# Three tiles of 128 rows in place of four in two input projections

## The reference, cut to what matters

```
# layer 0, per pixel                            # layer 1, per image
xn = layer_norm(x, ln1_w, ln1_b)                xn = normalise x in groups of channels over the image
xz = einsum('bld,ed->ble', xn, in_proj_w)       xz = W_in.T @ xn + b_in
xm, z = split(xz, 2)                            xm, z = split(xz, 2)
...  y * silu(z)                                ...  y * silu(z)
```

## Time and profile before

| | us |
|---|---|
| median of three runs | 18655.86 |
| lowest and highest run | 18643.19, 18657.38 |
| the profiled execution, from its first to its last instruction | 18660.7 |

### The profile page before, as it was taken

One profiled execution on the slowest core, in us unless ns is written; L12 is line 12 of the kernel. 1 busy time (PEld: TensorE's weight loads), 2 busy tenths in 40 slices (PEclk: granted clock), 3 DMA queues, 4 the chain that ended last, 5 costly groups with the idle time before them and its releaser, 6 DMA issues. The chain is left out here.

```text
span 18660.7 us, 271066 instructions
## 1 busy us (share of the span) xinstructions
PE 16820.2 (90%) x78344; PEld 10186.0 (55%) x78344; DVE 16050.6 (86%) x12158; ACT 15162.6 (81%) x24326; POOL 12567.1 (67%) x6247
## 2 busy tenths in 40 slices
PE   8799998899996798879899999999999999989798
PEld 3355554455552364455566666666666666547374
DVE  3799998899996486479899999999999999879698
ACT  7699996799992555557899999999999999845556
POOL 0099993599990474135799999999999999700101
PEclk9899998899997899999999999999999999999899
DMA  5788886788879677777433333333333333441313
GB/s 175 230 242 245 236 250 208 233 246 237 247 223 249 217 224 222 253 237 277 166 113 112 113 112 119 113 112 113 112 112 114 122 113 113 125 138 54 104 53 101
DMA packets 898273, 3166.02 MB, mean 170 GB/s; under 512 B 145638, under 2 KB 180170, under 8 KB 872140
## 3 DMA queue, kind: packets, MB, share of 16 engines
q1 hardware_dynamic: 817612, 3011.91, 51.1%
q10 hardware_dynamic: 79104, 136.10, 2.4%
HBM read 2342.21 MB, written 805.32 MB: 169 GB/s over the span
## 5 line engine op out<-in xcount | busy, mean ns | idle before, releaser
L1788 DVE TENSOR_TENSOR_SCAN l1s_h<-l1s_da,l1s_pd 128x1024 f32<-128x1024 f32 x3072 | 6778.1, 2268 | 241.5 <-PE l1s_pd L1720 163.4
L1831 ACT ACTIVATE l1s_dm<-l1s_dut,l1s_bt 128x384 f32<-128x384 f32 x7424 | 4056.8, 604 | 74.0 <-PE l1s_pd L1720 73.8
L1814 ACT ACTIVATE l1s_da<-l1s_dl,l1s_a 128x1024 f32<-128x1024 f32 x3072 | 3496.9, 1138 | 32.0 <-DVE l1s_h L1788 31.0
L1720 PE MATMUL l1s_pd<-l1s_id,l1s_dm 128*128 128x128 f32 x22272 | 2967.8, 274 | 36.4 <-DVE l1s_h L1788 33.9
L1720 PEld LDWEIGHTS l1s_pd<-l1s_id,l1s_dm 128*128 128x128 f32 x22272 | 2561.9, 142 | 487.7 <-issue 287.9
L1694 POOL TENSOR_TENSOR l1s_pb<-l1s_h,l1s_cc 128x1024 f32<-128x1024 f32 x1024 | 2517.8, 2459 | 95.0 <-DVE l1s_h L1788 83.4
L1698 POOL TENSOR_TENSOR l1s_pa<-l1s_sm,l1s_cc 128x1024 f32<-128x1024 f32 x1024 | 2433.1, 2376 | 0.0
L1731 PE MATMUL l1s_py<-l1s_pb,l1s_both 128*128 128x512 f32 x4096 | 2157.4, 609 | 197.1 <-POOL l1s_pb L1694 197.1
L1689 POOL TENSOR_TENSOR l1s_sm<-l1s_h 128x1024 f32<-128x1024 f32 x928 | 2203.5, 2374 | 122.8 <-DVE l1s_h L1788 122.6
L1731 PE MATMUL l1s_py<-l1s_pa,l1s_id 128*128 128x512 f32 x4096 | 2113.4, 598 | 0.3 <-POOL l1s_pa L1698 0.3
L2654 POOL TENSOR_TENSOR l0sf_pr<-l0sf_h,l0sf_cc 128x1024 f32<-128x1024 f32 x768 | 1813.8, 2380 | 71.1 <-DVE l0sf_h L2736 54.8
(11 more groups left out here) (318 smaller groups left out, 30375.1 us busy)
## 6 DMA issues: line engine op xcount, KB each, us to landing
l1s_cc<-crows SPq DMA_DIRECT2D x1024, 512.0 KB, 3.7
l0sf_cc<-l0crowsf SPq DMA_DIRECT2D x512, 512.0 KB, 5.5
l0sb_cc<-l0crowsb SPq DMA_DIRECT2D x512, 512.0 KB, 5.5
l0sf_cc<-l0crowsf SPq DMA_DIRECT2D x512, 256.0 KB, 7.1
l0sb_cc<-l0crowsb SPq DMA_DIRECT2D x512, 256.0 KB, 7.1
dls<-l1p_dl SPq DMA_DIRECT2D x192, 512.0 KB, 7.0
duts<-l1p_dut SPq DMA_DIRECT2D x64, 1536.0 KB, 5.9
l1s_dut<-duts SPq DMA_DIRECT2D x64, 1536.0 KB, 7.2
```

Source lines behind the costliest of these rows:

```text
L1720: mm = pe.transpose(pd[:, s % 2, blk * 128:blk * 128 + 128], dm[:, rnd % 2, blk, j * 128:j * 128 + 128], idt[:, :])
L1788: dve.tensor_tensor_scan(h[:, s % 4, :], da[:, j, :], pd[:, s % 2, :], 0.0, ALU.mult, ALU.add)\
L1814: act.activation(da[:, j, :], dl[:, half, j, :], ACT.Exp, scale=a[:, HT * half + j, n:n + 1])\
L1831: ins = act.activation(dm[:, rnd % 2, blk, :], dut[:, half, blk, :], ACT.Identity, scale=bt[:, half, blk, n:n + 1])
```

## The change

Both stages project their 384 rows as three tiles of 128: the first is xm rows 0 to 127, the last is z rows 64 to 191, and the middle one holds xm rows 128 to 191 in its lower 64 partitions and z rows 0 to 63 in its upper 64. Its two halves are taken out of PSUM by different engines.

In layer 0, ACT copies the first tile and applies Silu to the upper half of the second and to the third; the lower half of the second is a new `tensor_copy` on DVE, placed first in DVE's turn. PE's turn has projections 0 and 1, the average of squares, projection 2, the average of the image. The `pp` buffers are taken by (s + q) % 2, since three tiles a turn shift their parity.

```
@@ l0_in_proj
-        out = r.sb("out", [C, 2, 4, HW])
+        out = r.sb("out", [128, 2, 3, HW])
...
+                        to_x, to_z = xmp[s, :, bass.ds(c * HW + PAD, HW)], one(zs, FRAMES * s + c)
+                        for n, (done, at, dst, rows, q) in enumerate((
+                                (evac, 3 * k, to_x[0:DLOW], slice(0, 128), 0),
+                                (evacd, k, to_x[DLOW:DI], slice(0, DHIGH), 1),
+                                (evac, 3 * k + 1, to_z[0:DHIGH], slice(DHIGH, 128), 1),
+                                (evac, 3 * k + 2, to_z[DHIGH:DI], slice(0, 128), 2))):
+                            sp.wait_ge(done, nth(at))
...
                 def project(k, s, q):
-                    pe.wait_ge(evac, nth(4 * k + q - 2))
+                    pe.wait_ge(evac, nth((3 * k - 2, 3 * k - 1, 3 * k)[q]))
+                    if q == 0:
+                        pe.wait_ge(evacd, nth(k - 1))
...
-                        for q in range(2, 4):
-                            project(k, s, q)
+                        project(k, s, 2)
...
                 def turn(c, s):       # DVE
+                    k = c * SEQS + s
+                    if there(k):
+                        dve.wait_ge(proj, nth(3 * k + 1))
+                        dve.wait_ge(s_out[s % 2][1], (k - s % 2) * 8)
+                        dve.tensor_copy(out[0:DHIGH, s % 2, 1, :], pp[0:DHIGH, (s + 1) % 2, :]).then_inc(evacd, 1)
...
-                        for q in range(2):          # ACT
-                            evacuate(k, s, q)
+                        evacuate(k, s, 0, slice(0, 128), ACT.Copy)
...
-                        for q in range(2, 4):
-                            evacuate(k, s, q)
+                        evacuate(k, s, 1, slice(DHIGH, 128), ACT.Silu)
+                        evacuate(k, s, 2, slice(0, 128), ACT.Silu)
```

```
@@ l1_in_proj
-    OUTS = ((0, 128), (128, 128), (256, 128), (384, 64))
...
-                        for q in (0, 1):
-                            dve.wait_ge(proj, nth(4 * k + q))
+                        for q, rows in ((0, slice(0, 128)), (1, slice(0, DHIGH))):
+                            dve.wait_ge(proj, nth(3 * k + q))
...
                     def project(q):
-                        pe.wait_ge(evac, nth(2 * (k - 1) + q % 2))
-                        if q >= 2:
-                            pe.wait_ge(evacd, nth(2 * k + q % 2))
+                        if q < 2:
+                            pe.wait_ge(evac, nth(2 * (k - 1) + q))
+                        if q == 0:
+                            pe.wait_ge(evacd, nth(2 * (k - 1) + 1))
+                        if q == 2:
+                            pe.wait_ge(evacd, nth(2 * k))
...
                         project(2)
-                        project(3)
...
-                        for q in (2, 3):          # ACT
+                        for q, rows in ((1, slice(DHIGH, 128)), (2, slice(0, 128))):
@@ arranged
-    w["W_in"] = cat([wi[:, :DI], wi[:, DLOW:DI], wi[:, DI:]], 1)
-    w["b_in"] = cat([bi[:DI], bi[DLOW:DI], bi[DI:], np.zeros(64, f)]).reshape(4, 128).T
+    w["W_in"], w["b_in"] = wi, bi.reshape(3, 128).T
```

More of the change, by code:

```diff
@@ L178, in turn @@
                     if there(k):
-                        for q in range(4):
-                            sp.wait_ge(evac, nth(4 * k + q))
+                        to_x, to_z = xmp[s, :, bass.ds(c * HW + PAD, HW)], one(zs, FRAMES * s + c)
[5 more added lines that the diff above has]
+                            sp.wait_ge(done, nth(at))
                             sp.sem_inc(passed, 1)
[L182 to L185, removed]
+                            sp.dma_start(dst, out[rows, s % 2, q, :]).then_inc(s_out[s % 2][n], 16)
                         if there(k + SEQS):
@@ L204, in project @@
                 def project(k, s, q):
-                    pe.wait_ge(evac, nth(4 * k + q - 2))
+                    pe.wait_ge(evac, nth((3 * k - 2, 3 * k - 1, 3 * k)[q]))
+                    if q == 0:
+                        pe.wait_ge(evacd, nth(k - 1))
                     for hs in HALVES:
-                        mm = pe.matmul(pp[:, q % 2, hs], wt[:, q * C:(q + 1) * C], xn[:, s % 2, hs], start=True, stop=True)
+                        mm = pe.matmul(pp[:, (s + q) % 2, hs], wt[:, q * 128:q * 128 + 128], xn[:, s % 2, hs], start=True, stop=True)
                     mm.then_inc(proj, 1)
@@ L259, in _, with evacuate @@
                 act.wait_ge(const, nth(1))
[L261 to L264, removed]
+                def evacuate(k, s, q, rows, func):
+                    act.wait_ge(proj, nth(3 * k + q))
+                    act.wait_ge(s_out[s % 2][q + 1 if q else 0], (k - s % 2) * 8)
+                    act.activation(out[rows, s % 2, q, :], pp[rows, (s + q) % 2, :], func).then_inc(evac, 1)
                 def turn(c, s):
@@ L1237, in turn @@
                     if there(k):
-                        for q, (_, m) in enumerate(OUTS):
-                            sp.wait_ge(evacd if q < 2 else evac, nth(2 * k + q % 2))
+                        for n, (done, dst, rows, q) in enumerate((
+                                (evacd, xx[:, 0], slice(0, 128), 0), (evacd, xx[:, 1, 0:DHIGH], slice(0, DHIGH), 1),
+                                (evac, zs[:, 0:DHIGH, :], slice(DHIGH, 128), 1), (evac, zs[:, DHIGH:DI, :], slice(0, 128), 2))):
+                            sp.wait_ge(done, nth(2 * k + n % 2))
                             sp.sem_inc(passed, 1)
-                            dst = (one(xx[:, q], k) if q < 2 else
-                                   one(zs[:, 0:DLOW, :] if q == 2 else zs[:, DLOW:DI, :], k))
-                            sp.dma_start(dst, out[0:m, q, :]).then_inc(s_out[q], 16)
+                            sp.dma_start(one(dst, k), out[rows, q, :]).then_inc(s_out[n], 16)
                 turns(sp, turn, 3, 0, 2)
@@ L1265, in turn @@
                     if there(k):
-                        for q in (0, 1):
-                            dve.wait_ge(proj, nth(4 * k + q))
+                        for q, rows in ((0, slice(0, 128)), (1, slice(0, DHIGH))):
+                            dve.wait_ge(proj, nth(3 * k + q))
                             dve.wait_ge(s_out[q], k * 16)
-                            dve.tensor_scalar(out[:, q, :], pp[:, q % 2, :], bi[:, q:q + 1], None, ALU.add).then_inc(evacd, 1)
+                            dve.tensor_scalar(out[rows, q, :], pp[rows, (s + q) % 2, :], bi[rows, q:q + 1], None, ALU.add)\
+                               .then_inc(evacd, 1)
                     if there(k + 2):
@@ L1290, in project @@
                     def project(q):
-                        at, m = OUTS[q]
                         pe.wait_ge(xnd, nth(k))
-                        pe.wait_ge(evac, nth(2 * (k - 1) + q % 2))
-                        if q >= 2:
-                            pe.wait_ge(evacd, nth(2 * k + q % 2))
+                        if q < 2:
[4 more added lines that the diff above has]
+                            pe.wait_ge(evacd, nth(2 * k))
                         for hs in HALVES:
-                            mm = pe.matmul(pp[0:m, q % 2, hs], wi[:, at:at + m], xc[:, p, hs], start=True, stop=True)
+                            mm = pe.matmul(pp[:, (s + q) % 2, hs], wi[:, q * 128:q * 128 + 128], xc[:, p, hs], start=True, stop=True)
                         mm.then_inc(proj, 1)
@@ L1347, in turn @@
                     if there(k):
-                        for q in (2, 3):
[L1349 to L1352, removed]
+                        for q, rows in ((1, slice(DHIGH, 128)), (2, slice(0, 128))):
+                            act.wait_ge(proj, nth(3 * k + q))
+                            act.wait_ge(s_out[q + 1], k * 16)
+                            act.activation(out[rows, q, :], pp[rows, (s + q) % 2, :], ACT.Silu, bias=bi[rows, q:q + 1])\
+                               .then_inc(evac, 1)
                 turns(act, turn, 2, 0, 2)
```

14 lines of the change are left out of this document (7 added, 7 removed).

## The result

| | before | after |
|---|---|---|
| median, lowest to highest run (five each), us | 18643.19, 18633.34 to 18657.38 | 18720.1, 18686.12 to 18749.57 |
| ratio, 95% interval | | 1.0037, 1.0025 to 1.005 |
| span of the profiled execution, us | 18660.7 | 18747.8 |
| layer 0's input stage, us | 355.6 | 341.9 |
| layer 1's input stage, us | 495.0 | 563.5 |

The account below looks back on a forecast made before the run. Layer 0 was taken as bound by PE work, barely above its wait loop, layer 1 by its wait loop and clock losses. Layer 1's +64 and layer 0's -10 gave +54 on 18660.7, 18715; 18710 for the median, range 18664 to 18738.

Parts of the forecast that it names:

- Layer 0's turn, 10.0: Layer 0's input stage: a turn falls from 10.41 to 10.0 us, a gain of 12 us over 30 turns.
- the loop of waits: Layer 0: average of squares, Ln, Exp, table load, first Silu, next image's projections; 10.0 us a turn without Ln's delay.
- Ln's lateness: Layer 0: Ln waits for ACT's second Copy, 0.35 us a turn, which one Copy fewer removes.
- Layer 0's clock, +4: Layer 0: 1.4 us of PE idle a turn causes two or three clock losses in the stage, +4 us.
- Rival 4: Layer 0 loses the clock on each turn too, +39 - 2 in place of -10: 18757 us; chance 0.10.
- the 1.7 us forecast there: Layer 0's stage end: the last image's projections have four passes fewer on the path, 1.7 us gained.
- DVE's copy, 1.28, hidden: Layer 0: the new DVE copy takes 1.28 us, hidden because the multiply behind it waits for Exp.
- Layer 1's instructions, no gain of their own: Layer 1: four passes, 1.72 us a turn, go from beside the loop; only 1.7 us gained, in the last turn.
- Layer 1's clock, +2.8 on each of 29 turns: Layer 1: 3.7 us nearly idle on the PE loses the clock every turn; +66 us, +64 after the end gain.
- Rival 1: Layer 1: every turn loses the clock, but for 3.4 us only; +22 in all, 18678 us; chance 0.14.
- rival 2: Layer 1's clock holds as before, nine losses in 29 turns; 18642 us, not slower; chance 0.14.
- Rival 3: Both input stages: PE work is the bound, each removed pass comes off the time, 107 us; 18549 us; chance 0.04.

Follow-up runs that it names:

- The kernel with five products a turn: Changed kernel plus five unneeded 384-column matmuls per layer 1 turn, in the PE's idle time: 18718.36 us, ratio 1.0034 to before; layer 1's stage 479.2 us.
- the kernel with the Silu moved: Changed kernel with layer 1's table load and 64-row Silu ahead of ACT's accumulating sum: 18569.08 us, ratio 0.9964 to before; layer 1's stage 419.6 us.

## Why the prediction was right, point by point

The forecast was 18710 us, 54 above before; measured were 18720.1, 77 above before's median. By its steps:

- **Layer 0's turn, 10.0: right.** 10.08 over the stage, the loop of waits with Ln 0.04 behind the average, PE idle 1.25 us (said: 1.4). The gain is Ln's lateness, 0.3 to 0.4 us a turn, not the 1.7 us of PE work.
- **Layer 0's clock, +4: wrong in size.** No loss up to the last image: the granted clock is 1.00 over the stage. Rival 4 falls with it. Only the last image paid: its clock was at half for 6.8 us, before for 3.4. From the last average of squares to the stage's end it took 16.4 us, 16.7 before, and 14.7 in four kernels with the same code and 3.4 us at half. So of the 1.7 us forecast there 0.3 came. The stage's gain, 10 on the mean of six kernels each, is as forecast; the 13.7 of this pair have 3.3 from the clock in the first turn, which took 11.6 to 15.0 us with unchanged code.
- **DVE's copy, 1.28, hidden: right.** 1.22, and the multiply behind it still waits 2.82 us for Exp.
- **Layer 1's instructions, no gain of their own: right.** The mean's product stands straight behind the sum, the next projection still waits for the first Silu, and nothing on that loop became shorter. The two Silus take 2.25 us, as near to the 2.11 of before as was said.
- **Layer 1's clock, +2.8 on each of 29 turns: right.** 17.06 a turn is 2.87 above the 14.19. All 29 lost it, for 6.8 us, after 3.76 us with 0.33 of work (said: 3.7). Rival 1 (3.4 us at half) fails by the length of the slow stretches, rival 2 (the clock holds) by their number. The kernel with five products a turn shows that the clock is the cause and not merely beside it.
- **Rival 3, the PE's work as the bound: wrong**, since adding work helped. It is right about the kernel with the Silu moved, where little but PE work and the 1.16 us stop is left in a turn.
- **What no step had:** the edit moves all later code of the PE. Here it costs at most the 10 us by which the scan took longer (7223.1 for 7212.9), because its loop went from one fast place to another (28083 to 28003). That was luck: with layer 1's edit alone the scan would have put the same forecast 108 us too low.

The measured difference lies above the sum of the stages (55). The other 22 are within what the runs differ by, 18686 to 18750 after, and no row explains them; up to 10 may be the scan's. That the total came out 10 us from the forecast is in part chance.

## What to carry to other kernels

Before work is taken off an engine whose clock depends on how busy it is, see whether the time that goes lies on the loop of waits; if not, it becomes idle time, and the price is on all the work behind it. Then look for the order that closes the gap: here one Silu and its table load, moved out from behind the sum into the time in which ACT waited for the sum's input, turned 77 us slower into 75 us faster. And where an unchanged stage is slower, compare it around its jumps: the place of a loop in the program can be worth more than the change.

## What the runs showed of the hardware

- The clock can lock to a loop. In layer 1's stage 6.8 us at 1.2 GHz came back in every turn, behind 3.76 us with 0.33 of work; before, with 1.56 us of idle behind the small product, the clock fell in nine of 29 turns, for 3.4 us each. In layer 0's stage, with 1.25 us idle a turn, it did not fall before the last image.
- After a jump back the PE issued nothing for 2.5 to 2.75 us in the two kernels shown; at some places of the loop's start a second stop of some 2 us follows within three to seven matmul records, and a run of the loop takes 3.8 us or 1.7% more. The place repeats every 256 instructions, counted as the trace records them, and a transfer of 16384 bytes on the instruction queue begins around each second stop.
- The Trainium skill ("Runtime: NRT & Kernel Launch", section "Instruction fetch mechanics") says that a taken branch to code outside of what the engine holds has to fetch it first, in blocks of 256 instructions. The trace agrees with both: a stop behind each jump, and second stops at one point of 256 (219 + 9 and 211 + 17). That the PE waits for just that transfer is inferred from the times; no row names it.
